# Cross-attention and quantised feed-forward on one core: the weights' means one quad later, the weights' rounding spread over two quads

## The reference, cut to what matters

```python
x = x + xattn(ctx_1024, layernorm(x), mask, ...)      # 2048 rows of 256, 4 heads of 64
x = x + ffn(layernorm(x), w1, conv_w, conv_b, w2)     # hidden width 1024
# in ffn, for each of the two weight matrices:
def weight_quant(w):
    scale = 1.0 / clip(mean(abs(w)), 1e-5)
    return clip(round(w * scale), -1, 1) / scale
```

## Time and profile before

| what | before |
|---|---|
| median of 3 runs | 429.03 us (428.88 to 429.48) |
| profiled execution, own time | 430.1 us |
| its span | 428.3 us |
| PE busy | 406.1 us, 95% |
| DVE busy | 375.5 us, 88% |
| ACT busy | 314.7 us, 73% |
| POOL busy | 81.8 us, 19% |
| mean granted clock | 0.999 |

### The profile page before, as it was taken

One profiled execution on the slowest core, in us unless ns is written; L12 is line 12 of the kernel. 1 busy time (PEld: TensorE's weight loads), 2 busy tenths in 40 slices (PEclk: granted clock), 3 DMA queues, 4 the chain that ended last, 5 costly groups with the idle time before them and its releaser, 6 DMA issues.

```text
span 428.3 us, 14055 instructions
## 1 busy us (share of the span) xinstructions
PE 406.1 (95%) x6035; PEld 279.8 (65%) x6035; DVE 375.5 (88%) x595; ACT 314.7 (73%) x369; POOL 81.8 (19%) x109
## 2 busy tenths in 40 slices
PE   6999998999899999999999999999999998999885
PEld 6666675676567666666676666666676665676673
DVE  5889988988887899899799799799789899999994
ACT  2466777798979667766766767766766689999984
POOL 3387776101100020020020020020020010221200
PEclk9999999999999999999999999999999999999999
DMA  7825367112112112111111111111111000001002
GB/s 223 227 27 107 54 107 177 53 48 67 40 39 73 43 39 64 40 51 63 40 40 58 57 40 38 64 51 40 41 38 40 2 2 0 2 27 49 26 26 80
DMA packets 28687, 24.62 MB, mean 57 GB/s; under 512 B 6278, under 2 KB 28367, under 8 KB 28623
## 3 DMA queue, kind: packets, MB, share of 16 engines
q1 hardware_dynamic: 26106, 21.59, 15.7%
q0 software_dynamic: 2176, 2.10, 4.1%
q10 hardware_dynamic: 340, 0.01, 0.0%
HBM read 9.00 MB, written 2.10 MB: 26 GB/s over the span
## 4 chain that ended last, share of the span: by engine, by line
PE 49%; DVE 29%; ACT 16%; issue 4%; POOL 1%; DMA 1%; ACTq 0%; DVEq 0%
DVE arena L732 17%; PE sc L1742 11%; PE heads L1759 5%; ACT arena L1321 5%; PE heads L1760 4%; PE heads L1761 4%; PE heads L1567 3%; PE sc L1579 3%; ACT qq L1412 3%; PE by L1646 2%; ACT qq L1420 2%; PE sc L1846 2%; PE bx L1579 2%; PE by L1579 2%; ACT arena L1334 1%
## 5 line engine op out<-in xcount | busy, mean ns | idle before, releaser
L732 DVE SCALAR_TENSOR_TENSOR arena<-arena 128x1024 bf16<-128x1024 f32 x160 | 190.7, 1220 | 28.4 <-ACT arena L1321 27.3
L1321 ACT ACTIVATE arena<-sc,kb 128x1024 f32<-128x1024 f32 x160 | 170.0, 1114 | 58.0 <-PE sc L1742 57.9
L1759 PEld LDWEIGHTS heads<-v,arena 128*128 128x128 bf16 x1280 | 117.1, 97 | 40.3 <-issue 27.2
L1759 PE MATMUL heads<-v,arena 128*128 128x65 f16 x1280 | 129.7, 194 | 3.7 <-DVE arena L732 3.1
L1760 PE MATMUL heads<-v,arena 128*128 128x64 f16 x1280 | 128.9, 195 | 0.0
L1761 PE MATMUL heads<-v,arena 128*128 128x65 f16 x1280 | 128.3, 192 | 0.0
L1742 PE MATMUL sc<-qs,kst 64*128 64x512 f16 x960 | 118.0, 378 | 1.6 <-ACT arena L1321 0.9
L1760 PEld LDWEIGHTS heads<-v,arena 128*128 128x128 bf16 x1280 | 118.7, 97 | 0.1
L1761 PEld LDWEIGHTS heads<-v,arena 128*128 128x128 bf16 x1280 | 118.7, 99 | 0.0
L1742 PEld LDWEIGHTS sc<-qs,kst 64*128 64x128 f16 x960 | 40.1, 94 | 46.7 <-issue 3.5
L534 POOL TENSOR_SCALAR frs<-fmv 128x2 f32<-128x2 f32 x8 | 8.0, 996 | 221.2 <-DVE fmv L806 221.2
(11 more groups left out here) (209 smaller groups left out, 587.1 us busy)
## 6 DMA issues: line engine op xcount, KB each, us to landing
kst<-kk SPq DMA_DIRECT2D x80, 128.0 KB, 2.0
xs<-in_x SPq DMA_DIRECT2D x8, 256.0 KB, 5.2
xs<-in_L_xattn_b_out POOLq DMA_DIRECT2D x8, 256.0 KB, 6.0
qs<-qq SPq DMA_DIRECT2D x16, 128.0 KB, 2.4
out<-cbuf SPq DMA_DIRECT2D x7, 256.0 KB, 2.1
xs<-in_ctx SPq DMA_DIRECT2D x6, 256.0 KB, 6.1
xs<-in_L_ffn_w SPq DMA_DIRECT2D x1, 1024.0 KB, 6.0
cbuf<-in_L_ffn_w SPq DMA_DIRECT2D x1, 1024.0 KB, 9.2
```

The lines of the kernel that those rows point to most:

```text
L732: e.scalar_tensor_tensor(out=rest[:, j, :, :], in0=prob[:, j, :, :], scalar=SHRINK, in1=probh[:, j, :, :], op0=ALU.mult, op1=ALU.subtract) ...
L1321: a_.activation(prob[:, j, :, :], sc[(j + 1) % 2][:, :, :], ACT.Exp, bias=kb[:, bass.ds(i * QUAD + j, 1)]).then_inc(exp_done[j], 1)
L1759: t_.matmul(o, hi, row[:, 0:OW], start=first and sub == 0, stop=False, skip_group_check=True)
```

## The change

In the second unit DVE now takes the three remaining remainders of quad 5 in a row, then that of 6.0, then the means, then 6.1 to 6.3. On ACT the four roundings, which stood behind tiles 5.3, 6.1, 6.2 and 6.3, stand behind tiles 6.1, 6.2, 7.0 and 7.2. PE's, POOL's and SP's orders are unchanged.

```diff
@@ DVE, first_two_units
                 heads_weighed(0, 0, 0)
-                remainder(nq, 1)
+                for j in range(1, QUAD):
+                    remainder(nq, j)
+                remainder(nq + 1, 0)
                 weights_mean()
-                remainder(nq, 2)
-                remainder(nq, 3)
-                remainders(nq + 1)
+                for j in range(1, QUAD):
+                    remainder(nq + 1, j)
@@ ACT, first_two_units
                 exponentials(nq, 0)
-                weights_rounded(0, 0)
                 exponential(nq + 1, 1, 0)
                 exponential(nq + 1, 1, 1)
+                weights_rounded(0, 0)
+                exponential(nq + 1, 1, 2)
                 weights_rounded(0, 1)
-                exponential(nq + 1, 1, 2)
+                exponential(nq + 1, 1, 3)
+                exponential(nq + 2, 2, 0)
                 weights_rounded(1, 0)
-                exponential(nq + 1, 1, 3)
+                exponential(nq + 2, 2, 1)
+                exponential(nq + 2, 2, 2)
                 weights_rounded(1, 1)
-                over(2, nq - 2, lambda i: exponentials(nq + i, i))
+                exponential(nq + 2, 2, 3)
+                if isinstance(nq, int):
+                    over(3, nq - 2, lambda i: exponentials(nq + i, i))
...
```

More of the change, by code:

```diff
@@ L1359, in first_two_units @@
                 exponentials(nq, 0)
-                weights_rounded(0, 0)
                 exponential(nq + 1, 1, 0)
                 exponential(nq + 1, 1, 1)
+                weights_rounded(0, 0)
+                exponential(nq + 1, 1, 2)
                 weights_rounded(0, 1)
-                exponential(nq + 1, 1, 2)
+                exponential(nq + 1, 1, 3)
+                exponential(nq + 2, 2, 0)
                 weights_rounded(1, 0)
-                exponential(nq + 1, 1, 3)
+                exponential(nq + 2, 2, 1)
+                exponential(nq + 2, 2, 2)
                 weights_rounded(1, 1)
-                over(2, nq - 2, lambda i: exponentials(nq + i, i))
+                exponential(nq + 2, 2, 3)
+                if isinstance(nq, int):
+                    over(3, nq - 2, lambda i: exponentials(nq + i, i))
+                else:
+                    with act.If(nq > XP // 2 + 1):
+                        over(3, nq - 2, lambda i: exponentials(nq + i, i))
                 for w in range(2):
```

## The result

| | before | changed |
|---|---|---|
| median | 429.00 us (21 runs, 428.62 to 430.85) | 429.73 us (21 runs, 429.37 to 430.93) |
| ratio to before | | 1.0019, 95% interval 1.0013 to 1.0025 |
| span of the profiled execution | 428.3 us | 428.0 us |

The changed kernel is 0.19% slower, 0.8 us: just inside the 0.2% that was called no change, on the slow side of it. The interval leaves no doubt of the sign, but it reaches past 0.2%, so on which side of that edge the true value lies is open. The forecast was 429.6, in the range of 428.6 to 430.2.

What follows compares the result with a forecast made beforehand. PE was taken to bound unit 1, so only its waits count: -0.53 at the means, +1.12 at the first two roundings, +0.03 in quad 7, in all +0.62 us on 429.03, giving 429.6; range 428.6 to 430.2.

Steps and rivals of the forecast that it cites:

- The hold on the remainders: DVE, quad 5: POOL's L558 and L559 hold the remainders of 5.2 and 5.3 by 0.40 and 0.85 us.
- the sign: DVE, quad 5: the remainders of 5.1 to 5.3 were to take 4.75 us instead of 3.49.
- PE at 5.3: PE, values of 5.3: of 1.04 us lost at the means 0.51 stays lost; PE is 0.53 ahead of before.
- ACT's new wait: ACT, before the first rounding: a new wait of 1.48 us for the means, until 112.71.
- The score of 7.1: PE: this score starts at 117.14 instead of 116.55, leaving PE 0.59 us behind before.
- Quad 7: PE, quad 7: a 0.34 us wait at the score of 8.1 replaces 0.31 at the values of 7.3, +0.03.
- Rival 1: DVE, quad 5: POOL doesn't hold remainders; PE ends +0.07, time 429.1; chance 0.25.
- Rival 2: DVE, quad 5: POOL's instructions hold for their whole length, 0.55 and 1.17 us; price +1.09, time 430.1; chance 0.12.
- Rival 3: PE: the losses of 1.04 at the means and 0.50 at the roundings both go; time 427.5; chance 0.04.
- Rival 4: Whole kernel: program and code placement moves the time some tenths either way, within the runs' spread; others' chance 0.04.

Runs made afterwards that it cites:

- kernel 8: Kernel before, with roundings behind 6.1, 6.3, 7.1 and 7.3 and POOL's split of the output weights behind the second clip: 426.90 us, ratio 0.9948.
- kernel 2: Kernel before, with POOL's split of the output weights waiting for the second clip of the weights: 428.46 us, ratio 0.9989.
- kernel 1: Changed kernel, with POOL's split of the output weights waiting for the second clip of the weights: 429.20 us, ratio 1.0001.
- Kernel 7: Changed kernel, with DVE's means behind 5.3 and ACT's roundings behind 6.1, 6.3, 7.1 and 7.3: 427.53 us, ratio 0.9966.
- kernel 5: Changed kernel, with the second, third and fourth roundings moved behind 6.3, 7.1 and 7.3: 428.61 us, ratio 0.9995.
- kernel 4: Changed kernel, with POOL's L559 replaced by a memset to zero, so the output weights' low half is missing: 429.27 us, ratio 1.0006.

## Why the prediction was right

- **The hold on the remainders.** Predicted 0.40 for 5.2 and 0.85 for 5.3, by what L745 and L749 had lost. Measured 1.63 - 1.22 = 0.41 and 2.17 - 1.22 = 0.95. The second term was 0.10 too small. I had taken off 0.17 us, from what a POOL instruction of two numbers needs after release, and that was too much; with 0.95 the same working gives +0.72, with +0.77 measured. The three remainders 5.1 to 5.3 took 4.86 us against the 4.75 named as the sign.
- **PE at 5.3.** 0.51 of loss predicted, none at 5.2. The recorded idle time is 0.49, but the prediction counted from start to start, against PE's pace: the pairs of scores of 6.0 and 6.2 start at 107.58 and 111.23, 3.65 apart instead of 2.98, so 0.67 is lost (before: 108.38 and 112.39, 1.03). PE was 0.36 ahead of before here, not 0.53.
- **ACT's new wait.** 1.48 predicted. The recorded idle time is 1.47; counted from starts, as the prediction did, it is 1.59 (112.04 less 108.45 and two steps of 1.00). The 0.10 of L559 is in it too.
- **The score of 7.1.** Predicted 0.59 behind before. Measured 116.47 against 116.56 less the 0.80 of start-up, 0.71 behind: the 0.10 of L559 and 0.02. So 0.36 gained and 1.07 waited away, for the 0.53 and 1.12 of the sum; the two errors partly cancel.
- **Quad 7.** Predicted +0.03, measured +0.06 (0.77 less 0.71). That everything behind keeps its pace is borne out by the medians, 0.73 apart; that this agrees with the stretch within 0.04 is in part luck, as the other kernels' differ by up to 0.29 and before's own median was 428.98, 429.00 and 429.18 in three sets.
- **Rival 1** (no hold on the remainders) fell by the lengths of 5.2 and 5.3. What spoke for it, the remainder of 5.1 that took 1.22 us beside L557, was misread: L557's recorded 1.53 us isn't the time in which it holds. In kernel 8, where L557 came in between two remainders, it held the second one for 0.41 (1.63), like L558. In kernel 2 a remainder that started 0.47 us behind L557 (127.22 against 126.75) took its 1.23, and in kernel 1 one that started 0.66 behind it did too. L557's hold is over by then, and in before 5.1 started 0.84 behind it.
- **Rival 2** (POOL holds for its whole recorded length) would have made 5.2 take 1.77 and 5.3 2.39. They took 1.63 and 2.17.
- **Rival 3** (the gain of 1.0 and 0.5) failed for the reason given: exponential 6.2 is queued behind the waiting rounding. Kernel 7, at -1.37, shows that most of it was to be had by other places of the same instructions.
- **Rival 4** (placement of the program) has nothing to explain here: stalls that the rows show account for the 0.77 of the stretch. No run tested it by itself.
- **The chances.** Slower by over 0.2% was given 0.20 and within 0.2% 0.74. The result, 0.17 to 0.19%, sits near that edge; of what brought it there, 0.10 is L559's. That it fell inside is luck, since the interval spans the edge.

The Trainium skill's rule ("SBUF — State Buffer", section "Who interferes with whom") names the pairs that the trace shows: a remainder with two SBUF inputs and a `tensor_scalar` were held by POOL's reading instructions, and a POOL memset held nothing that it ran beside. Its "for the whole instruction" agrees with the trace only if the instruction's own reads are meant (0.41 and 0.95 us), not the recorded lengths (0.92 and 1.17).

## What to carry to other kernels

Before moving a slow instruction, ask why it is slow: L749 took 1.08 us only because POOL worked beside it, and moving it away handed a hold to the instructions that took its place. To say what such a hold is worth to a change, take it away from both kernels and not from one: 0.12 is left with it gone from the changed kernel alone, 0.84 with it gone from both. A wait that is moved behind an engine's queue has to be followed to the next engine: of the 1.04 us lost at the means 0.36 was gained, and PE's waits for ACT gave back 1.07. Where PE takes tiles in pairs, side work did better behind a whole pair than between its two tiles: 1.19 us in kernel 5 against the changed kernel.

## What the runs showed of the hardware that I had not expected

- The hold was of one size where the next remainder followed at once: 0.41 us for a POOL instruction that reads 128x512 numbers once (L558 in the changed kernel and in kernels 1 and 4, L557 in kernel 8; 0.44 for L558 in kernel 2), 0.95 for one that reads two such inputs (L559 in the changed kernel and kernel 8). A remainder that starts later loses only what is left: after an idle time of 0.24 us in kernel 1 and 0.20 in kernel 2, those beside L559 took 1.87 and 1.91, 0.65 and 0.69 more than 1.22. A POOL memset of 128x512 cost DVE nothing visible.
- DVE's recorded length of an instruction contains the time for which it is held (1.63, 2.17 us), while its idle time shows nothing. In the changed kernel the busy time of DVE grew by 0.31 us in the stretch without any more work.
- The part ahead of the change varies between profiled executions by more than the whole effect: the scores of 5.2 began at 104.24 us in kernel 5 and at 105.38 in before, and the same eight products took 1.99 and 2.63 us in two of them. For an effect of tenths, two profiles were comparable only from the first instruction of the changed stage on.
